# A four-part hybrid layer on one core: row variances of the feed-forward outputs on GpSimd, and every feed-forward sum begun in PSUM by VectorE

## The chip, the core and the metric

The kernel runs on one core of a Trainium2 chip. The metric is device time in microseconds (us) of one launch, the median of three runs. Everything is float32. The engines are TensorE (PE in the profile), VectorE (DVE), ScalarE (ACT), GpSimd (POOL) and SyncE (SP).

## The reference, cut to what matters

```python
def _layernorm(x, eps=1e-5):  m, v = mean(x), var(x); return (x - m) / sqrt(v + eps)
def attn(h):                  q = h @ Wq.T; return (q @ h.T) @ h            # no softmax
def ffn(t):                   x = t + relu(t @ w1[0] + b1[0]) @ w2[0] + b2[0]
                              return (x - mean(x)) * rsqrt(var(x) + 1e-5) * gamma + beta
def mix(x):                   ...   # RWKV time mixing (a scan over tokens), then channel mixing
x = hidden                                    # 8 batches of 512 rows x 128 columns
x = x + attn(_layernorm(x))
x = x + ffn(_layernorm(x))                    # called f1 in the kernel
x = x + mix(_layernorm(x))                    # called tmix and cmix in the kernel
x = x + ffn(_layernorm(x))                    # f2, with the same weights as f1
```

The feed-forward part keeps expert 0 alone, since the reference sets its weight to one. Its input t is a normed row, and its own result is normed again after t, the product and b2 are added up.

## The kernel before, in words

A tile is one of the eight batches: 512 rows, laid as 4 blocks (j) of 128 rows with 128 columns each. All eight tiles of x stay in SBUF (R0 to R7). Each tile goes through five parts: attention, f1, tmix, cmix, f2. Nothing is scheduled by a compiler: each engine has a list of calls written out by hand, in which parts of different tiles are interleaved, and each call waits on counting semaphores for what it needs. The lists end the functions of each engine. An engine takes its list strictly in order.

One feed-forward tile runs so. `normed` (ScalarE, L828) writes the normed rows `y`; `ffn_transpose` (TensorE, L1114) turns them, ScalarE copies them to `yT` (L881, L884); `hidden_up` (L1155) multiplies by W1 into four banks of PSUM, `relu` (L895) moves these to `h`. Then z = y + h @ W2 + b2 is summed up in one PSUM bank: the bank is begun with y and `ffn_down` (L1164) adds 16 products to it. There are two ways to begin it.

- Tiles in `STARTED` (f1: 0 to 3, f2: 4 to 7): VectorE's `ffn_start` (L700; for the last tile `last_start`, L707, in two halves) writes y + B2R into the bank; B2R is b2 less its mean, in every row.
- The other eight tiles: TensorE's `ffn_start` (L1275) transposes yT back into the bank, in four steps, where yT holds y + B2C since ScalarE adds the column B2C as it copies (L884). Their hidden layer takes the bias B1C = B1 - W1.T B2C instead of B1; `bias_part` (L1267) and `up_bias` (L733) make B1C once.

W2 is centred at the start (`centre_down_weights`), y is centred, and so is b2 in either form: every row of z has mean zero. The norm of z thus needs the variance alone. `z_stats` (VectorE, L440) takes `bn_stats` of the four blocks, `mean_var` (VectorE, L523) aggregates these, `z_log` (L1012) and `z_root` (L1017) on ScalarE make rs = (var + eps) ** -0.5, and `ffn_scaled` (VectorE, L560) writes zg = z * rs * gamma, which frees the bank. GpSimd adds zg to R by a DMA that accumulates (`ffn_sum`, L382), after it has added beta in the same way (`ffn_residual`, L374). Tile 0 of f1 is added by VectorE (`ffn_gain` L538, `ffn_out` L546), the last of f2 in two halves by `last_stats` to `last_out`.

The other names that the prediction uses: `gated` (VectorE, L650) is the last step of a tile's time mixing before its output product `product_o` (TensorE, L1213); `tmix_out` (L658) adds this product; `cmix_out` (L691) ends tile 7's channel mixing on VectorE. `bias_diagonal` (L717), `bias_rows` (L1258, L1259) and `bias_rows_centred` (L722 to L727) make B2R and B2C at the start. `shift`, `power` and `bias` are the three GpSimd steps of the other norms (L293, L294, L346, L350), with small 128x4 operands.

## Time and profile before

| | us |
|---|---|
| median of 3 runs | 259.32 (259.31 to 259.61) |
| the profiled execution's own time | 259.21 |
| its span, from first to last instruction | 257.4 |

| engine | busy us | share | instructions |
|---|---|---|---|
| TensorE, matmuls | 249.5 | 97% | 1504 |
| VectorE | 231.2 | 90% | 757 |
| ScalarE | 231.9 | 90% | 477 |
| GpSimd | 133.2 | 52% | 258 |

The profile comes from one execution. 1.8 us of its time lie outside the span. A matmul of float32 appears as two instructions, a transpose as one. Instructions overlap on one engine: the next starts before the one before it has ended. So what an instruction costs an engine without idle time is the distance from its start to the next start, which is shorter than its duration. DMA issues on GpSimd (L374, L382, L390, L397) take its time as well.

### The profile page before, as it was taken

To read this page: it belongs to the slowest core of one execution; us is meant where nothing else is said; L and a number is where in the kernel's file an instruction comes from. 1 tells how busy PE (TensorE), PEld (TensorE's weight loads), DVE (VectorE), ACT (ScalarE), POOL (GpSimd) and SP (SyncE) were. 2 spreads that over 40 slices of the span, in tenths; PEclk is the share of its full clock that TensorE was granted. 3 is DMA by queue.
4 is the path that set the end of the run, shared out by engine and by line. 5 is a ranking of instruction groups with operands and counts; after the bars stand their busy time and mean duration, and the time that the engine had idled before them with its cause. 6 is when DMAs were issued, how large, how long until landed. Compare 5 with 4: busy or idle time off the path is not lost.

```text
span 257.4 us, 5284 instructions
## 1 busy us (share of the span) xinstructions
PE 249.5 (97%) x1504; PEld 187.8 (73%) x1504; DVE 231.2 (90%) x757; ACT 231.9 (90%) x477; POOL 133.2 (52%) x258
## 2 busy tenths in 40 slices
PE   7899999999999999999999999999999999999991
PEld 7687778768767777668759767757848849778771
DVE  5897999999999999999999999999999995955454
ACT  3789789999999999999999999999999999895741
POOL 1656585944961974044596646636604525340640
PEclk9999999999999999999999999999999999999998
DMA  7932224013022240020763422205204424374297
GB/s 196 308 99 45 42 42 84 0 28 56 3 40 43 41 84 1 0 45 0 134 105 52 74 48 45 42 0 98 67 0 85 81 56 70 55 144 87 45 187 179
DMA packets 17772, 18.10 MB, mean 70 GB/s; under 512 B 1488, under 2 KB 11600, under 8 KB 17744
## 3 DMA queue, kind: packets, MB, share of 16 engines
q0 software_dynamic: 6480, 11.80, 27.0%
q1 hardware_dynamic: 10848, 5.84, 8.1%
q8 instruction: 12, 0.20, 0.3%
q10 hardware_dynamic: 416, 0.14, 0.2%
q14 instruction: 16, 0.13, 0.2%
HBM read 3.87 MB, written 2.10 MB: 23 GB/s over the span
## 4 chain that ended last, share of the span: by engine, by line
PE 94%; DVE 2%; DMA 1%; ACT 1%; POOL 1%; issue 0%; DVEq 0%; POOLq 0%; ACTq 0%
PE bank L1155 21%; PE bank L1164 21%; PE bank L1232 11%; PE bank L1226 11%; PE bank L1114 7%; PE bank L1213 3%; PE bank L1243 3%; PE bank L1197 3%; PE bank L1207 3%; PE bank L1202 3%; PE bank L1142 3%; PE bank L1127 2%; PE bank L1275 1%; DMA R<-in_hidden 1%; PE bank L1175 1%; PE bank L1135 1%
## 5 line engine op out<-in xcount | busy, mean ns | idle before, releaser
L1164 PEld LDWEIGHTS bank<-W,f_h 128*128 128x128 f32 x480 | 58.2, 192 | 8.7 <-issue 8.6
L1155 PE MATMUL bank<-f_yT,W 128*128 128x512 f32 x128 | 61.2, 593 | 0.0
L1164 PE MATMUL bank<-W,f_h 128*128 128x128 f32 x480 | 60.2, 275 | 0.0
L1155 PEld LDWEIGHTS bank<-f_yT,W 128*128 128x128 f32 x128 | 21.9, 190 | 16.3 <-issue 11.3
L1232 PEld LDWEIGHTS bank<-FWv,KK 128*128 128x128 f32 x256 | 30.6, 192 | 3.4 <-issue 2.3
L1226 PE MATMUL bank<-XK,FWk 128*128 128x512 f32 x64 | 32.0, 597 | 0.0
L1232 PE MATMUL bank<-FWv,KK 128*128 128x128 f32 x256 | 31.8, 275 | 0.0
L828 ACT ACTIVATE f_y<-R,f_yn_nb,f_yn_rs 128x128 f32<-128x128 f32 x64 | 26.3, 490 | 0.9 <-POOL f_yn_nb L350 0.9
L895 ACT ACTIVATE f_h<-bank,B 128x512 f32<-128x512 f32 x32 | 21.2, 681 | 5.5 <-PE bank L1155 4.2
L390 POOL DMA_DIRECT2D R<-G x7 | 6.3, 897 | 36.4 <-DVE G L686 36.4
L895 ACT ACTIVATE f_h<-bank,B1C 128x512 f32<-128x512 f32 x32 | 21.4, 682 | 0.1
L293 POOL TENSOR_TENSOR f_yn_ve<-f_yn_mv,K_EPS 128x4 f32<-128x4 f32 x16 | 7.9, 493 | 25.6 <-DVE f_yn_mv L523 25.5
L382 POOL DMA_DIRECT2D R<-f_zg x14 | 14.1, 1006 | 13.4 <-DVE f_zg L560 11.2
L956 ACT ACTIVATE KK<-KK 128x512 f32<-128x512 f32 x32 | 19.8, 637 | 0.0
L952 ACT ACTIVATE KK<-bank 128x512 f32<-128x512 f32 x32 | 18.8, 599 | 0.8 <-PE bank L1226 0.7
L346 POOL TENSOR_TENSOR f_yn_rs<-f_yn_ve,K_RSQRT 128x4 f32<-128x4 f32 x16 | 19.3, 1206 | 0.0
L560 DVE SCALAR_TENSOR_TENSOR f_zg<-bank,f_zn_rs,GAMMA 128x128 f32<-128x128 f32 x56 | 15.6, 338 | 3.2 <-issue 2.2
L374 POOL DMA_DIRECT2D R<-BETA x16 | 15.7, 1037 | 4.6 <-ACT f_y L828 4.0
L1226 PEld LDWEIGHTS bank<-XK,FWk 128*128 128x128 f32 x64 | 10.7, 190 | 8.2 <-issue 4.4
L440 DVE BATCH_NORM_STATS2 f_zn_stats<-bank 128x6 f32<-128x128 f32 x60 | 13.1, 279 | 1.7 <-PE bank L1164 1.7
L440 DVE BATCH_NORM_STATS2 f_yn_stats<-R 128x6 f32<-128x128 f32 x64 | 13.7, 275 | 0.1
L828 ACT ACTIVATE N<-R,tmix_nb,tmix_rs 128x128 f32<-128x128 f32 x32 | 13.2, 489 | 0.4 <-POOL tmix_nb L350 0.4
(159 smaller groups left out, 620.3 us busy)
## 6 DMA issues: line engine op xcount, KB each, us to landing
R<-BETA POOLq DMA_DIRECT2D x16, 256.0 KB, 3.6
R<-f_zg POOLq DMA_DIRECT2D x14, 256.0 KB, 4.0
R<-N POOLq DMA_DIRECT2D x8, 256.0 KB, 3.4
R<-in_hidden SPq DMA_DIRECT2D x7, 256.0 KB, 5.0
R<-G POOLq DMA_DIRECT2D x7, 256.0 KB, 3.4
out_x<-R SPq DMA_DIRECT2D x7, 256.0 KB, 2.3
W<-in_w SPq DMA_DIRECT2D x2, 256.0 KB, 4.5
BETA<-in_beta SPq DMA_DIRECT2D x1, 256.0 KB, 4.6
```

Source lines behind the costliest of these rows:

```text
L346: pool.tensor_tensor(n.rs[b % 2][:], n.ve[b % 2][:], K_RSQRT[:], ALU.pow).then_inc(n.scale.sem(b), 1)
L374: pool.dma_start(R[b][:], BETA[:], accum_op=ALU.add).then_inc(*f.xb.step(b))
L440: last = v.bn_stats(n.stats[b % 2][:, j, :], src[:, j, :])
L828: done = a.activation(dst[:, j, :], src[:, j, :], ACT.Identity, scale=n.rs[b % 2][:, j:j + 1], bias=n.nb[b % 2][:, j:j + 1])
L895: a.activation(at(f.h, b)[:, n, :], banks[bank][:], ACT.Relu, bias=bias[:, n:n + 1]).then_inc(f.h_ready[n], 1)
L952: a.activation(at(KK, b)[:, n, :], banks[bank][:], ACT.Relu).then_inc(square[n].sem(b), 1)
L956: a.activation(at(KK, b)[:, n, :], at(KK, b)[:, n, :], ACT.Square).then_inc(square[n].sem(b), 1)
L1114: last = t_.matmul(banks[bank][:, j * P:(j + 1) * P], src[:, j, :], IDENT[:], start=(j == 0), stop=(j == J - 1), is_transpose=True, skip_g ...
L1155: t_.matmul(banks[bank][:], W1[:, n * P:(n + 1) * P], at(f.yT, b)[:], start=True, stop=True).then_inc(f.h_psum[n], 1)
L1164: last = t_.matmul(banks[bank][:, j * C:(j + 1) * C], at(f.h, b)[:, n, j * P:(j + 1) * P], W2[:, n, :], start=False, stop=(n == H - 1), sk ...
L1226: t_.matmul(banks[bank][:], FWk[:, n * P:(n + 1) * P], at(XK2, b)[:], start=True, stop=True).then_inc(kk_psum[n], 1)
L1232: last = t_.matmul(banks[bank][:, j * C:(j + 1) * C], at(KK, b)[:, n, j * P:(j + 1) * P], FWv[:, n, :], start=(n == 0 and j == 0), stop=(n ...
```

## The change

Four edits, and new orders of the calls on all five engines.

1. `STARTED` now names all sixteen tiles. VectorE's `ffn_start` runs for f1 4 to 7 and f2 0 to 3 too; TensorE's `ffn_start`, `bias_part` and VectorE's `up_bias` are called no more.
2. `mean_var` is no longer called for the z of 15 tiles (all but the last one's halves). GpSimd's new `z_spread` takes the sums of squares out of the `bn_stats` results instead: a group of 128 columns gives two means (even and odd columns) and two sums of squares about them. Since the whole row's mean is zero, 128 times the variance is the sum of the latter two less 128 times the product of the two means. These are four 128x4 instructions.
3. `z_log` waits for `z_spread` and scales by 1/128 as it takes the logarithm.
4. `bias_diagonal` and `bias_rows` stand ahead of tile 0's attention, and tile 0's `attn_gram` ahead of its transpose.

```diff
-STARTED = {"f1": (0, 1, 2, 3), "f2": (4, 5, 6, 7)}
+STARTED = {"f1": tuple(range(BATCHES)), "f2": tuple(range(BATCHES))}
...
+            def z_spread(b, n):
+
+                pool.wait_ge(n.stats_done, b + 1)
+                if b >= 2:
+                    pool.wait_ge(*n.scale.done(b - 2, "ve"))
+                st = n.stats[b % 2]
+                pool.tensor_tensor(n.pair[b % 2][:], st[:, :, 1], st[:, :, 4], ALU.mult).then_inc(n.scale.sem(b), 1)
+                pool.tensor_tensor(n.sum[b % 2][:], st[:, :, 2], st[:, :, 5], ALU.add)
+                pool.wait_ge(*n.scale.done(b, "pair"))
+                pool.tensor_tensor(n.pair[b % 2][:], n.pair[b % 2][:], K_C[:], ALU.mult).then_inc(n.scale.sem(b), 1)
+                pool.wait_ge(*n.scale.done(b, "scaled"))
+                pool.tensor_tensor(n.spread[b % 2][:], n.sum[b % 2][:], n.pair[b % 2][:], ALU.subtract).then_inc(n.scale.sem(b), 1)
...
             def row_stats(b, n, src):
                 if b >= 2:
-                    dve.wait_ge(n.mv_ready, b - 1)
+                    if n in (f1.znorm, f2.znorm):
+                        dve.wait_ge(*n.scale.done(b - 2, "spread"))
+                    else:
+                        dve.wait_ge(n.mv_ready, b - 1)
...
             def z_log(b, f):
                 n = f.znorm
-                act.wait_ge(const_ready, 8)
-                act.wait_ge(n.mv_ready, b + 1)
+                act.wait_ge(const_ready, 9)
+                act.wait_ge(*n.scale.done(b, "spread"))
...
+                a.activation(n.ve[b % 2][:], n.spread[b % 2][:], ACT.Ln, bias=K_EPS[:, 0:1], scale=1.0 / C).then_inc(n.scale.sem(b), 1)
...
-            warm_up(0, 10)
...
-            ffn_down(0, f1, 0, 3); ffn_down(0, f1, 1, 3); ffn_down(0, f1, 2, 3); ffn_down(0, f1, 3, 3)
...
+            bias_rows(); attn_gram(0, 0); attn_transpose(0, 1); attn_proj(0, 0); attn_apply(0, 0)
```

Where the orders differ is seen in three places. Line numbers of after are those of the changed file.

VectorE from the first `bn_stats` of an f1 sum (tile 0, f1_zn_stats0) on; before:

```order
L440 BN_STATS f1_zn_stats0<-bank3 128x6 x4
L523 BN_AGGR f1_zn_mv0<-f1_zn_stats0 128x2 x4
L538 TENSOR_TENSOR f1_zg0<-bank3,GAMMA 128x512
L546 SCALAR_TENSOR_TENSOR R0<-f1_zg0,f1_zn_rs0,R0 128x128 x4
L440 BN_STATS tmix_stats0<-R0 128x6 x4
L523 BN_AGGR tmix_mv0<-tmix_stats0 128x2 x4
L529 TENSOR_TENSOR R3<-bank2,R3 128x512
L756 TENSOR_SCALAR WROW<-WROW,WDEC 128x512
L440 BN_STATS f1_yn_stats1<-R3 128x6 x4
L440 BN_STATS attn_stats1<-R7 128x6 x4
```

and after, from the two rows ahead of it:

```order
L464 BN_STATS attn_stats1<-R7 128x6 x4
L729 TENSOR_TENSOR bank4<-f1_y1,B2R 128x512
L464 BN_STATS f1_zn_stats0<-bank2 128x6 x4
L567 TENSOR_TENSOR f1_zg0<-bank2,GAMMA 128x512
L575 SCALAR_TENSOR_TENSOR R0<-f1_zg0,f1_zn_rs0,R0 128x128 x4
L464 BN_STATS tmix_stats0<-R0 128x6 x4
L547 BN_AGGR tmix_mv0<-tmix_stats0 128x2 x4
L729 TENSOR_TENSOR bank7<-f1_y2,B2R 128x512
L558 TENSOR_TENSOR R3<-bank2,R3 128x512
L464 BN_STATS f1_yn_stats1<-R3 128x6 x4
```

The aggregation of z is gone, and tile 7's attention statistics have moved ahead of z's.

VectorE at the end of tile 7's time mixing (`gated` is the row G<-EA,G); before:

```order
L631 TENSOR_TENSOR AB<-AB,EB 128x2x512
L636 TENSOR_TENSOR EA<-AB,EA 128x1024
L642 SCALAR_TENSOR_TENSOR G<-G,EA 128x512
L681 SCALAR_TENSOR_TENSOR G2<-bank5,G2 128x512
L646 SCALAR_TENSOR_TENSOR G<-bank4,G 128x512
L686 TENSOR_TENSOR G2<-bank0,G2 128x512
L650 TENSOR_TENSOR G<-EA,G 128x512
L677 SCALAR_TENSOR_TENSOR DC<-DC,VEC,XC 128x512
L700 TENSOR_TENSOR bank2<-f2_y1,B2R 128x512
L523 BN_AGGR f2_zn_mv0<-f2_zn_stats0 128x2 x4
L658 SCALAR_TENSOR_TENSOR N1<-N1,tmix_back1,bank6 128x128 x4
```

and after:

```order
L660 TENSOR_TENSOR AB<-AB,EB 128x2x512
L695 TENSOR_TENSOR DC<-XC 128x512
L665 TENSOR_TENSOR EA<-AB,EA 128x1024
L702 SCALAR_TENSOR_TENSOR XK2<-DC,VEC,XC 128x512
L671 SCALAR_TENSOR_TENSOR G<-G,EA 128x512
L710 SCALAR_TENSOR_TENSOR G2<-bank3,G2 128x512
L675 SCALAR_TENSOR_TENSOR G<-bank5,G 128x512
L715 TENSOR_TENSOR G2<-bank2,G2 128x512
L679 TENSOR_TENSOR G<-EA,G 128x512
L706 SCALAR_TENSOR_TENSOR DC<-DC,VEC,XC 128x512
L729 TENSOR_TENSOR bank3<-f2_y1,B2R 128x512
L687 SCALAR_TENSOR_TENSOR N1<-N1,tmix_back1,bank4 128x128 x4
```

Two steps of channel mixing now stand between instructions that need each other's result; the `ffn_start` behind `gated` was there before.

TensorE about tile 7's `product_o` (the row with Wo); before:

```order
L1226 MATMUL bank6<-XK2,FWk 128x512
L1226 MATMUL bank5<-XK2,FWk 128x512
L1155 MATMUL bank4<-f2_yT0,W1 128x512
L1155 MATMUL bank0<-f2_yT0,W1 128x512
L1213 MATMUL bank6<-Wo,G 128x128 x4
L1155 MATMUL bank7<-f2_yT0,W1 128x512
L1243 MATMUL bank0<-FWr,DC 128x128 x4
```

and after:

```order
L1257 MATMUL bank1<-XK2,FWk 128x512
L1257 MATMUL bank3<-XK2,FWk 128x512
L1257 MATMUL bank5<-XK2,FWk 128x512
L1257 MATMUL bank2<-XK2,FWk 128x512
L1244 MATMUL bank4<-Wo,G 128x128 x4
L1186 MATMUL bank1<-f2_yT0,W1 128x512
L1195 MATMUL bank3<-W2,f2_h 128x128 x4
L1274 MATMUL bank4<-FWr,DC 128x128 x4
```

The same products stand ahead of it and behind it as before, in another order.

## Rows read from the trace of the kernel before

**Rows 1.** The page: busy us of each engine, and the chain that ended last.
```profile
PE 249.5 (97%) x1504; PEld 187.8 (73%) x1504; DVE 231.2 (90%) x757; ACT 231.9 (90%) x477; POOL 133.2 (52%) x258
PE 94%; DVE 2%; DMA 1%; ACT 1%; POOL 1%; issue 0%; DVEq 0%; POOLq 0%; ACTq 0%
```
**Rows 2.** Windows: stretch, its us, busy us and instructions of PE, PEld, DVE, ACT, POOL; clock.
```profile
0.00:26.00 26.00, 23.38 (x151) 20.25 (x152) 19.53 (x108) 18.86 (x48) 13.18 (x48) 1.00 0.60 160
26.00:210.50 184.50, 184.47 (x1086) 134.86 (x1085) 183.21 (x530) 180.07 (x358) 102.50 (x183) 1.00 0.27 48
211.50:257.40 45.90, 40.67 (x267) 32.26 (x265) 27.45 (x120) 31.96 (x70) 16.55 (x28) 0.98 0.57 110
```
**Rows 3.** VectorE in order of time, 204 to 213 us: start, duration, instruction.
```profile
204.99 1.22 DVE L631 TENSOR_TENSOR AB<-AB,EB 128x1024 f32<-128x1024 f32 x1
206.25 1.23 DVE L636 TENSOR_TENSOR EA<-AB,EA 128x1024 f32<-128x1024 f32 x1
...
210.28 0.69 DVE L650 TENSOR_TENSOR G<-EA,G 128x512 f32<-128x512 f32 x1
210.89 0.74 DVE L677 SCALAR_TENSOR_TENSOR DC<-DC,VEC,XC 128x512 f32<-128x512 f32 x1
211.56 0.69 DVE L700 TENSOR_TENSOR bank<-f_y,B2R 128x512 f32<-128x512 f32 x1
212.16 0.37 DVE L523 BATCH_NORM_AGGREGATE f_zn_mv<-f_zn_stats 128x2 f32<-128x6 f32 x4
```
**Rows 4.** TensorE in order of time, 204 to 213 us.
```profile
204.77 0.60 PE L1114 MATMUL bank<-IDENT,f_y 128*128 128x128 f32 x4
205.21 1.91 PE L1226 MATMUL bank<-XK,FWk 128*128 128x512 f32 x4
...
211.54 1.05 PE L1213 MATMUL bank<-Wo,G 128*128 128x128 f32 x8
```
**Rows 5.** TensorE in order of time, 13 to 48 us.
```profile
13.79 0.39 PE L1258 MATMUL bank<-DIAG,MEAN 128*128 128x128 f32 x2
...
14.15 1.14 PE L1142 MATMUL bank<-PROJ,XNT 128*128 128x128 f32 x8
...
21.58 0.60 PE L1114 MATMUL bank<-IDENT,f_y 128*128 128x128 f32 x4
22.06 3.81 PE L1164 MATMUL bank<-W,f_h 128*128 128x128 f32 x32
...
46.31 0.95 PE L1267 MATMUL bank<-B2C,W 128*128 128x1 f32 x8
47.12 1.10 PE L1207 MATMUL bank<-DX,Wr 128*128 128x512 f32 x2
```
**Rows 6.** VectorE in order of time, 25 to 38 us.
```profile
25.91 0.89 DVE L440 BATCH_NORM_STATS2 f_zn_stats<-bank 128x6 f32<-128x128 f32 x4 [1.67 <-PE bank L1164]
26.83 0.38 DVE L523 BATCH_NORM_AGGREGATE f_zn_mv<-f_zn_stats 128x2 f32<-128x6 f32 x4
27.13 0.66 DVE L538 TENSOR_TENSOR f_zg<-bank,GAMMA 128x512 f32<-128x512 f32 x1
27.88 1.14 DVE L546 SCALAR_TENSOR_TENSOR R<-f_zg,f_zn_rs,R 128x128 f32<-128x128 f32 x4
...
35.47 0.66 DVE L567 TENSOR_TENSOR DX<-XA 128x512 f32<-128x512 f32 x1
36.17 0.75 DVE L573 SCALAR_TENSOR_TENSOR XK<-DX,VEC,XA 128x512 f32<-128x512 f32 x1
36.84 1.12 DVE L560 SCALAR_TENSOR_TENSOR f_zg<-bank,f_zn_rs,GAMMA 128x128 f32<-128x128 f32 x4
```
**Rows 7.** GpSimd in order of time, 30 to 36 us.
```profile
30.41 0.20 POOL L328 TENSOR_TENSOR tmix_tmp<-tmix_mv,K_EPS 128x4 f32<-128x4 f32 x1 [2.67 <-DVE tmix_mv L523]
30.57 0.20 POOL L329 TENSOR_TENSOR tmix_nm<-tmix_mv,K_NEG 128x4 f32<-128x4 f32 x1
...
32.66 0.89 POOL L374 DMA_DIRECT2D R<-BETA  x1
...
34.34 1.05 POOL L293 TENSOR_TENSOR f_yn_ve<-f_yn_mv,K_EPS 128x4 f32<-128x4 f32 x1
```
**Rows 8.** ScalarE in order of time, 27 us.
```profile
27.31 0.30 ACT L1012 ACTIVATE f_zn_ve<-f_zn_mv,K_EPS 128x4 f32<-128x4 f32 x1 [1.52 <-DVE f_zn_mv L523]
27.64 0.20 ACT L1017 ACTIVATE f_zn_rs<-f_zn_ve 128x4 f32<-128x4 f32 x1
```
**Rows 9.** Line L650, all eight: duration ns min/median/max.
```profile
L650 DVE TENSOR_TENSOR G<-EA,G x8: 658/663/693, 56.9 to 210.3; 128x512 f32<-128x512 f32 x8
```

More of the change, by code:

```diff
@@ L139, in __init__ @@
                 self.rs = copies(n + "_rs", [P, J], 2)
+                if "spread" in steps:
+                    self.pair, self.sum, self.spread = (copies(n + "_" + m, [P, J], 2) for m in ("pair", "sum", "spread"))
                 self.stats_done = sem(n + "_stats_done")
@@ new lines, in _ @@
+            mean_var(1, f2.norm); with_current(4); tmix_change(5); mean_var(6, nt); gate_sum(4); cmix_change(3)
+            mix_k(5); z_stats(7, f1, 2); cmix_k(3); gate_log(4, 5); running_max(5, 7); cgate_log(2, 1); gated(4)
+            ffn_start(1, f2, 1, cgate.done(2, "rl")); differences(5, 7); mix_v(5); cmix_gated(2, 0); mix_r(5)
+            tmix_out(4, 5); z_stats(0, f2, 3); cmix_stats(4); cmix_r(3); mean_var(4, ncm); ffn_stats(2, f2)
+            new_values(5, 4); ffn_scaled(7, f1, 2); tmix_change(6); denominator_sum(5); mean_var(2, f2.norm)
@@ new lines, in _ @@
+            first_values(5, 4); numerator_sum(5); mix_k(6); weighted(5); with_current(5); cmix_change(4); gate_sum(5)
+            cmix_k(4); mix_v(6); tmix_stats(7); gate_log(5, 7); cgate_log(3, 2); mean_var(7, nt); gated(5)
+            running_max(6, 7); cmix_gated(3, 5); differences(6, 7); tmix_out(5, 6)
+            ffn_start(2, f2, 0, square[1].done(4, "relu")); cmix_stats(5); ffn_scaled(0, f2, 3); mean_var(5, ncm)
+            ffn_stats(3, f2); mix_r(6); cmix_r(4); new_values(6, 7); mean_var(3, f2.norm); first_values(6, 7)
@@ new lines, in _ @@
+            denominator_sum(7); numerator_sum(7); weighted(7); cmix_change(6); with_current(7); cmix_k(6); gate_sum(7)
+            cgate_log(5, 3); gate_log(7, 5); cmix_gated(5, 2); gated(7); cmix_r(6)
+            ffn_start(4, f2, 3, square[0].done(6, "relu")); tmix_out(7, 4); cmix_stats(7); mean_var(7, ncm)
+            ffn_stats(5, f2); z_stats(3, f2, 7); mean_var(5, f2.norm); cmix_change(7); cmix_k(7); cgate_log(6, 4)
+            z_stats(4, f2, 3); cmix_r(7); ffn_scaled(2, f2, 0); cmix_gated(6, 6)
@@ L819, in _ @@
+            last_scaled(1, 7); last_out(0); last_out(1)
         @block.scalar
@@ L1097, in _ @@
+            relu(7, f2, 3, 6); relu(7, f2, 0, 2); z_log(6, f2); z_root(6, f2.znorm); relu(7, f2, 1, 5)
+            relu(7, f2, 2, 6); last_log(0); last_root(0); last_log(1); last_root(1)
         @block.tensor
```

524 lines of the change are left out of this document (249 added, 275 removed).

## The prediction, made before the changed kernel ran

> **What bounds the kernel now.** I read the page's busy times and chain first [rows 1]. They seem to say it all: TensorE is busy for 249.5 of 257.4 us and holds 94% of the chain that ended last. But the chain only says that TensorE never had to wait at the end of a step; two other engines are at 90%. So I read windows next [rows 2]. From 26 to 210.5 us TensorE is busy for 184.47 of 184.50 us, and VectorE for 183.21, ScalarE for 180.07. Three engines are full there, and the kernel before is a balance of three. After 211.5 us VectorE has 27.5 us of work in 45.9, ScalarE 32.0, TensorE 40.7: there TensorE alone is full.
>
> Third, I looked in order of time for the place where one kind of bound hands over to the other. VectorE's `gated` of tile 7 starts at 210.28 and the instruction behind it at 210.89; it ends at 210.97 [rows 3]. TensorE starts `product_o` of tile 7, which needs it, at 211.54 [rows 4]. The slack between them is 0.57 us, all that TensorE's queue is behind VectorE at this point. From there to the end it takes 257.4 - 211.54 = 45.9 us, of which 40.7 are TensorE's own work without a gap.
>
> So the end is: the start of `product_o` of tile 7, plus 45.9 us, if what TensorE has behind it stays the same. And its start is the later of two: TensorE's own work ahead, and VectorE's work up to `gated` (with ScalarE's, whose full stretch is as long).
>
> **The change part by part: TensorE.** It loses 8 times four transposes back. Four transposes take 205.21 - 204.77 = 0.44 us from start to start [rows 4], so 8 x 0.44 = 3.5. It loses `bias_part`, 47.12 - 46.31 = 0.8 us [rows 5]. Together 4.3 us, and all of it ahead of `product_o` of tile 7. Behind that call the new order has the same calls in both kernels: gate 7 and gate 6, the downs of f2 4, all of f2 5 to 7 and of cmix 7, the last hidden piece of f2 4. Taken alone this would let `product_o` start at 207.2.
>
> **VectorE, up to `gated` of tile 7.** I counted the calls ahead of it in both orders. Added: 8 `ffn_start`. One costs 212.16 - 211.56 = 0.60 us from start to start [rows 3], so +4.8. Removed: `mean_var` of ten z, f1 0 to 7 and f2 0 and 1 (the other five stand behind `gated`, where VectorE has time to spare), and `up_bias`, one 128x4 instruction of some 0.05. A `mean_var` costs 27.13 - 26.83 = 0.30, so ten are -3.0. All else ahead of `gated` is the same. The sum is +1.75 us: on the engine that is full from 26 to 211 us the change is a loss, since it takes out fewer short instructions there than it puts in long ones.
>
> The new order gives some of it back. Where an instruction needs the result of the one just ahead of it, it starts after that one's end: L636 starts at 206.25, 0.04 after 204.99 + 1.22. Where it doesn't, it starts before the end: L700 at 211.56, 0.07 before 210.89 + 0.74 [rows 3]. Such a pair costs 0.11 to 0.12 us. From `ffn_out` of tile 0 to `gated` of tile 7 I count 16 such pairs before and 8 after (in the second piece of the orders DC and XK2 have been put between three of them). That is 8 x 0.12 = -1.0.
>
> The start of this stretch, in three steps. (a) The bias products (14.15 - 13.79 = 0.36 us [rows 5]) move to where TensorE still waits for tile 0, and two of the four downs of f1 0 no longer wait for a relu behind the transposes of tile 1. Before, the ups end just ahead of the transposes that start at 21.58, the downs run from 22.06 and z_stats begins at 25.91 [rows 5, 6]. After, with 3.6 us of downs and 0.44 of transposes from 21.6 on, it begins at 25.6: -0.3. (b) From z_stats to `ffn_out` it was 27.88 - 25.91 = 1.97 us [rows 6]. Now GpSimd stands between. Its independent instructions start 0.15 us apart and end 0.20 after their start [rows 7], so `z_spread` of four, with two waits on itself of about 0.1, takes 0.8 us. From the start of z_log to that of `ffn_out` it was 27.88 - 27.31 = 0.57 [rows 6, 8]. With two handovers of 0.1: 25.6 + 0.9 + 0.1 + 0.8 + 0.1 + 0.6 = 28.1, so `ffn_out` starts 0.2 later than before, and VectorE idles 0.9 us ahead of it. (c) Behind `ffn_out` stand +4.8 for 8 starts, -2.7 for nine `mean_var`, -0.05, -0.8 for tile 7's attention statistics, which have moved ahead of z_stats into idle time (first piece of the orders), and +0.3 for tile 6's aggregation, which has moved behind it. That makes +1.55, and +0.55 with the pairs.
>
> `gated` of tile 7 then starts at 210.28 + 0.2 + 0.55 = 211.0 and ends at 211.7. `product_o` starts as soon as the signal is there, at 211.8, for TensorE has been waiting: 211.8 - 211.54 = +0.3. The 4.3 us taken from TensorE turn into idle time ahead of that. The end: 259.21 + 0.3 = 259.5 for an execution like the profiled one, which lies 0.1 below the median of 259.32. Against the median I forecast 259.6, and all times below are against it.
>
> **ScalarE** has the same instructions; one more relu and two fewer of cmix stand ahead of its last step for tile 7's gate. I cost it at nothing. Its cover is VectorE's own length, and if VectorE were faster, ScalarE with 180 of 184.5 us would be next.
>
> **GpSimd** gets 15 x 4 instructions. At 0.2 us each they are 12 us, 133 to 145 of 257, on an engine with gaps. The work hides, the latency need not: z_log on ScalarE and behind it `ffn_scaled` on VectorE, each with a full queue behind it, now wait for it. The shortest cover is f1 tile 1, where between z_stats and `ffn_scaled` stand the decay row, tmix_change and mix_k, some 0.5 + 0.7 + 0.67 = 1.9 us (the latter two from 35.47 to 36.84 [rows 6]), against the chain of 1.8. All others have 4 us or more. But GpSimd is not even: behind a DMA issue the same 128x4 addition took 1.05 instead of 0.20 us [rows 7]. Bounds for this wait, summed over 14 tiles: 0 if every cover holds, 14 x 0.85 = 12 us if each z_spread met such a delay without cover. I take 0 on top of tile 0's, since the covers of 4 us are above 1.8 + 2 x 0.85.
>
> VectorE's eight new starts read two tiles of SBUF. L650 does the same, and its eight took 658 to 693 ns while GpSimd was busy for 55% of the stretch [rows 2, 9]: nobody holds VectorE up. The Trainium skill (SBUF — State Buffer, "Who interferes with whom") says that a VectorE instruction with two SBUF inputs and a GpSimd instruction that reads SBUF share a read port, and whichever comes second is blocked until the first is done. By that rule each new GpSimd instruction could hold a VectorE instruction for up to its own 0.2 us; with some 40 of them ahead of `gated` and about half of VectorE's time in such instructions that would be an estimated 4 us, and 263.6 in all. The spread of 35 ns in rows 9 speaks against it for VectorE; the long GpSimd rows would be the other side of it.
>
> **The rivals.**
> A. Faster, by VectorE. Its stretch has more waste to give than my 8 pairs: it is 184.4 us from z_stats to `gated`, of which by my count 16 pairs x 0.12 and six waits of about 0.18 for other engines were waste, 3 us. With TensorE early, results lie ready and these waits (1.1 us) go too, and if tile 0's wait of 0.9 is shorter than I think, another 0.5. `gated` 1.6 earlier than forecast: 258.0. With the rest of the 3 us gone as well (2.0 behind the 1.0 that I count, and 0.3 of pairs at the start) 257.3.
> B. Faster, by TensorE: it was the bound after all, and the whole 4.3 us come out: 255.0. For it speaks the chain's 94%. Against it speaks that VectorE has no gap to shrink.
> C. Slower, by the new wait: `z_spread` comes late, because GpSimd stands in its order at a DMA issue or at a wait for someone else, and VectorE and ScalarE, both full, stand still behind `ffn_scaled` and `z_log`. It decides from the second such stall on: each costs its full length, 0.5 to 1 us. With three of 0.8: 262.0. For it: 15 new chains through an engine in strict order, whose instructions vary by a factor of five. Against: 39 norms went the same way before.
> D. Slower, by the clock. TensorE now idles 4 to 5 us ahead of 211.8. In the last stretch, where it stops some 5 us before the end, the granted clock was 0.98 on average [rows 2], so it fell from 2.4 towards 1.2 GHz there. If the idle time came in one piece, 4 us of products at half speed cost 4 us: 263.6. The Trainium skill (TensorE: Matmul & The Clock Gate, "What's actually happening") has the same: the clock is given by activity and taken back when idle. Spread over many waits, as up to 26 us where it stayed at 1.00 with 2.6 us of idle time, it costs nothing.
>
> **How the numbers follow.** Forecast (259.6, own range 258.8 to 260.4): 0.45. A 0.24, B 0.04, C 0.23, D 0.04. Differences below 0.2%, 0.5 us, can't be told from none here. The middle of the forecast's range lies within 258.8 to 259.8: I give 0.30 to same, 0.11 to slower and 0.04 to faster of its 0.45. A goes to faster but for 0.05, B to faster, C and D to slower: faster 0.27, same 0.35, slower 0.38. The range for 8 in 10 goes from 257.4 (within A; beyond it 0.08) to 262.0 (C as priced; beyond it 0.09).
>
> **What would show it.** Right: TensorE has some 4 us of waits between 26 and 212 us, most ended by VectorE; VectorE is busy without a gap over it; L679 starts at about 211.0 and L1244 at 211.8; from there to the end 45.9. Step (b) is right if VectorE idles 0.9 us ahead of L575. C would show as idle time of VectorE ahead of L589, ended by f_zn_rs, and of ScalarE ahead of f_zn_ve, ended by POOL. B would be right if VectorE had gaps and L679 started near 207. The forecast is wrong if the stretch behind `product_o` is not the same 45.9, for then the hand-over lies elsewhere.

## The result: 262.1 us, slower by 2.7, and the profile after

| | before | after |
|---|---|---|
| median, us | 259.31 | 262.06 (261.91 to 263.21, four runs) |
| profiled execution, its span | 259.21, 257.4 | 262.12, 260.3 |
| VectorE starts `ffn_out` of tile 0 | 27.88 | 27.93 |
| VectorE starts `gated` of tile 7 | 210.28 | 213.26 |
| TensorE starts `product_o` of tile 7 | 211.54 | 214.51 |
| from there to the end of the span | 45.9 | 45.8 |

The ratio is 1.0108, with an interval of 1.0089 to 1.0126: slower, and just outside the range that I gave.

The page of after, busy us and the chain that ended last. Before, TensorE held 94% of the chain [rows 1].

```profile
PE 249.0 (96%) x1464; PEld 182.6 (70%) x1464; DVE 230.5 (89%) x704; ACT 232.1 (89%) x477; POOL 152.3 (59%) x319
PE 55%; DVE 16%; ACT 12%; issue 8%; POOL 6%; DMA 1%; DVEq 0%; ACTq 0%; POOLq 0%
```

The chain now passes from engine to engine. Windows of after, with the columns of [rows 2] (behind the clock stand the DMA engines' share and GB/s):

```profile
26.00:211.50 185.50, 181.84 (x1041) 129.08 (x1039) 182.02 (x493) 178.62 (x355) 115.55 (x219) 1.00 0.26 48
211.50:260.30 48.80, 43.71 (x274) 33.54 (x272) 28.30 (x104) 34.82 (x76) 22.19 (x49) 0.97 0.51 103
```

The clock is 1.00 up to 211.5 us. In this stretch TensorE now idles 3.7 us, VectorE 3.5 and ScalarE 6.9, where it was 0.0, 1.3 and 4.4 [rows 2]. VectorE at the start of its full stretch, after (before: [rows 6]):

```profile
25.52 0.89 DVE L464 BATCH_NORM_STATS2 f_zn_stats<-bank 128x6 f32<-128x128 f32 x4 [1.79 <-PE bank L1195]
...
27.93 1.14 DVE L575 SCALAR_TENSOR_TENSOR R<-f_zg,f_zn_rs,R 128x128 f32<-128x128 f32 x4 [0.93 <-ACT f_zn_rs L1048]
...
34.14 0.89 DVE L464 BATCH_NORM_STATS2 f_zn_stats<-bank 128x6 f32<-128x128 f32 x4 [0.86 <-PE bank L1195]
...
35.73 0.69 DVE L596 TENSOR_TENSOR DX<-XA 128x512 f32<-128x512 f32 x1 [0.31 <-ACT XA L927]
```

The first two rows are steps (a) and (b) of the prediction, and they came as forecast: they start at 25.52 and 27.93 us, where I had said 25.6 and 28.1, and the wait is 0.93 us, where I had said 0.9. The other two waits are new. And VectorE and TensorE at the hand-over, after (before: [rows 3, 4]):

```profile
213.26 0.69 DVE L679 TENSOR_TENSOR G<-EA,G 128x512 f32<-128x512 f32 x1
```
```profile
210.95 3.72 PE L1257 MATMUL bank<-XK,FWk 128*128 128x512 f32 x8
214.51 1.05 PE L1244 MATMUL bank<-Wo,G 128*128 128x128 f32 x8
```

`product_o` starts 1.25 us after `gated`, by the same distance as before (1.26), and right behind TensorE's other work. So TensorE had not run ahead at all, though 4.3 us of work were taken from it.

**How TensorE's lost time is read.** The page hardly shows it: 40 instructions went, and its busy time fell by 0.5 us, since the modelled ends of matmuls cover short waits. The starts show it. In a stretch without waits a 128x512 matmul starts 0.43 us after the one before, a 128x128 one 0.11. Here is one of the two largest gaps of after (the other, at 121.6 us, is as long):

```profile
97.20 1.16 PE L1263 MATMUL bank<-FWv,KK 128*128 128x128 f32 x8
99.07 1.10 PE L1228 MATMUL bank<-XK,Wk 128*128 128x512 f32 x2 [0.71 <-DVE XK L602]
```

Eight starts at 0.11 end at 98.1; the product starts at 99.07, so nearly 1 us is lost where the row says 0.71. Summed over all starts from 26 to 212 us, TensorE lost 1.3 us before and 9.1 us after. That is 7.8 more against 4.3 of work saved: +3.5, of which `product_o` of tile 7 shows 3.0 (in the two orders TensorE also stands at different calls at 26 us). The same sum on VectorE, over distances that exceed the usual one of the same instruction by more than 0.2 us, is 0.2 us in one place before and 3.3 in six places after. Its small gaps of 0.05 to 0.2 us, among them the dependent pairs of the prediction, fell from about 3 us to about half of that. These sums are mine, from the starts in the traces; I call them lost time below.

### The profile page after: what moved, and what is told of

Same layout as the page of the kernel before. It is cut to its first block, busy times and chain, and to the rows that moved or that the text cites. A ratio compares the mean times of both kernels' runs of the same rounds, so it can differ in the third digit from the quotient of the medians.

```text
span 260.3 us, 5233 instructions
## 1 busy us (share of the span) xinstructions
PE 249.0 (96%) x1464; PEld 182.6 (70%) x1464; DVE 230.5 (89%) x704; ACT 232.1 (89%) x477; POOL 152.3 (59%) x319
## 3 DMA queue, kind: packets, MB, share of 16 engines
q0 software_dynamic: 6480, 11.80, 25.6%
## 4 chain that ended last, share of the span: by engine, by line
PE 55%; DVE 16%; ACT 12%; issue 8%; POOL 6%; DMA 1%; DVEq 0%; ACTq 0%; POOLq 0%
PE bank L1186 13%; PE bank L1195 13%; PE bank L1263 8%; PE bank L1257 6%; PE bank L1145 4%; PE bank L1228 2%; DVE f_zg L589 2%; PE bank L1274 2%; ACT EA L944 2%; PE bank L1173 1%; PE bank L1158 1%; DVE AB L655 1%; PE bank L1244 1%; ACT EA L952 1%; ACT EB L939 1%
## 5 line engine op out<-in xcount | busy, mean ns | idle before, releaser
L1195 PE MATMUL bank<-W,f_h 128*128 128x128 f32 x480 | 61.2, 276 | 0.1
L919 ACT ACTIVATE f_h<-bank,B 128x512 f32<-128x512 f32 x64 | 42.5, 681 | 7.1 <-PE bank L1186 6.1
L1257 PE MATMUL bank<-XK,FWk 128*128 128x512 f32 x64 | 31.1, 597 | 0.0
L399 POOL DMA_DIRECT2D R<-f_zg x14 | 13.2, 942 | 12.7 <-DVE f_zg L589 11.5
L297 POOL TENSOR_TENSOR f_yn_ve<-f_yn_mv,K_EPS 128x4 f32<-128x4 f32 x16 | 9.5, 592 | 18.9 <-DVE f_yn_mv L547 18.9
L589 DVE SCALAR_TENSOR_TENSOR f_zg<-bank,f_zn_rs,GAMMA 128x128 f32<-128x128 f32 x56 | 15.5, 338 | 5.4 <-issue 5.4
L391 POOL DMA_DIRECT2D R<-BETA x16 | 17.6, 1097 | 4.3 <-ACT f_y L852 3.7
L976 ACT ACTIVATE KK<-bank 128x512 f32<-128x512 f32 x32 | 18.0, 596 | 0.3 <-PE bank L1257 0.3
L363 POOL TENSOR_TENSOR f_yn_rs<-f_yn_ve,K_RSQRT 128x4 f32<-128x4 f32 x16 | 18.0, 1127 | 0.0
L332 POOL TENSOR_TENSOR tmix_tmp<-tmix_mv,K_EPS 128x4 f32<-128x4 f32 x8 | 2.3, 290 | 23.6 <-DVE tmix_mv L547 23.6
L852 ACT ACTIVATE NC<-N,cmix_nb,cmix_rs 128x128 f32<-128x128 f32 x32 | 13.2, 485 | 0.7 <-POOL cmix_nb L367 0.6
```

The costliest lines, as they stand in the source:

```text
L363: pool.tensor_tensor(n.rs[b % 2][:], n.ve[b % 2][:], K_RSQRT[:], ALU.pow).then_inc(n.scale.sem(b), 1)
L391: pool.dma_start(R[b][:], BETA[:], accum_op=ALU.add).then_inc(*f.xb.step(b))
L589: last = v.scalar_tensor_tensor(zg[:, j, :], z[:, j, :], f.znorm.rs[b % 2][:, j:j + 1], GAMMA[:], ALU.mult, ALU.mult)
L852: done = a.activation(dst[:, j, :], src[:, j, :], ACT.Identity, scale=n.rs[b % 2][:, j:j + 1], bias=n.nb[b % 2][:, j:j + 1])
L919: a.activation(at(f.h, b)[:, n, :], banks[bank][:], ACT.Relu, bias=bias[:, n:n + 1]).then_inc(f.h_ready[n], 1)
L976: a.activation(at(KK, b)[:, n, :], banks[bank][:], ACT.Relu).then_inc(square[n].sem(b), 1)
```

## The experiments

All were timed beside the kernel before, in five groups (its median was 259.25 to 259.52 in them). A difference between two runs of different groups can be off by up to 0.3 us for that reason alone; the ratios are each taken within a group. Lists of calls in the cuts below are wrapped anew, so that both sides show the same calls. "Old" and "new orders" are the call lists of the kernel before and of the changed one. "Lost" is TensorE's from 26 to 212 us; `gated` is tile 7's start.

| run | orders | sums begun by | z variance | us | ratio to before | `gated` | lost |
|---|---|---|---|---|---|---|---|
| before | old | both | VectorE | 259.3 | 1 | 210.3 | 1.3 |
| after | new | VectorE | GpSimd | 262.1 | 1.0108 | 213.3 | 9.1 |
| e1 | new | VectorE | VectorE | 263.4 | 1.0147 (1.0128 to 1.0166) | 214.2 | 9.7 |
| e2 | new | VectorE | left out | 261.1 | 1.0061 (1.0045 to 1.0077) | 211.9 | 7.6 |
| e3 | new | both | GpSimd | 262.0 | 1.0097 (1.0081 to 1.0113) | 213.7 | 5.0 |
| e4 | new | both | VectorE | 262.5 | 1.0123 (1.0105 to 1.0141) | 213.8 | 5.0 |
| e5 | old | VectorE | GpSimd | 266.5 | 1.0276 (1.0260 to 1.0292) | 217.1 | 12.5 |
| e6 | old | both | GpSimd | 262.1 | 1.0104 (1.0088 to 1.0121) | 212.2 | 3.8 |
| e7 | old | VectorE | VectorE | 265.4 | 1.0229 (1.0212 to 1.0247) | 215.5 | 10.8 |
| e8 | old | both | left out | 258.6 | 0.9973 (0.9962 to 0.9984) | 210.1 | 0.7 |
| e9 | old | transposes left out | VectorE | 259.2 | 0.9997 (0.9983 to 1.0010) | 210.0 | 4.8 |
| e10 | old | transposes left out | left out | 258.2 | 0.9966 (0.9950 to 0.9981) | 209.1 | 4.0 |
| e11 | new | transposes left out | VectorE | 261.9 | 1.0100 (1.0083 to 1.0117) | 213.2 | 7.5 |
| e12 | old | both | GpSimd for 6 tiles | 258.0 | 0.9948 (0.9930 to 0.9966) | 209.4 | 0.8 |
| e13 | new | both | left out | 261.8 | 1.0090 (1.0072 to 1.0107) | 212.9 | 4.3 |
| e14 | old | both | GpSimd for 2 tiles | 260.6 | 1.0042 (1.0027 to 1.0057) | 212.3 | 3.5 |
| e15 | new | VectorE | GpSimd for 12 tiles | 261.1 | 1.0055 (1.0042 to 1.0069) | 213.2 | 8.6 |
| e16 | new, one place put back | both | VectorE | 263.9 | 1.0176 (1.0160 to 1.0191) | 214.9 | 6.3 |
| e17 | the same | VectorE | GpSimd for 12 tiles | 264.7 | 1.0199 (1.0181 to 1.0216) | 217.3 | 12.1 |

**Undoing the parts in the new orders: e1 to e4.** e1 puts `mean_var` back behind each `z_stats` and drops `z_spread`:

```diff
-                act.wait_ge(*n.scale.done(b, "spread"))
+                act.wait_ge(n.mv_ready, b + 1)
...
-            z_stats(1, f1, 4); decay_along_tokens(); tmix_change(0); mix_k(0)
+            z_stats(1, f1, 4); decay_along_tokens(); mean_var(1, f1.znorm); tmix_change(0); mix_k(0)
```

> The changed kernel with part 2 undone: mean_var of all fifteen z is back on VectorE, right behind z_stats (one call later where that is possible), z_log reads it again, GpSimd has no z_spread. Orders otherwise those of the changed kernel. The changed kernel takes 262.1. V (VectorE's length sets the time): ten aggregations of 0.30 come back ahead of gated of tile 7, so 264 to 265. G (the new steps on GpSimd hold the other norms and z up, and these waits are the loss): VectorE's waits of 1.9 us go and pay for most of the 3.0, ScalarE's waits for POOL go too: 261 to 262.5. O (the new orders are the loss, TensorE and VectorE wait for each other by turns): about 262 to 263, with the waits of TensorE unchanged.

e2 leaves the variance out:

```diff
-                a.activation(n.ve[b % 2][:], n.spread[b % 2][:], ACT.Ln, bias=K_EPS[:, 0:1], scale=1.0 / C).then_inc(n.scale.sem(b), 1)
+                a.activation(n.ve[b % 2][:], n.stats[b % 2][:, :, 2], ACT.Ln, bias=K_EPS[:, 0:1], scale=2.0 / C).then_inc(n.scale.sem(b), 1)
```

> The changed kernel, orders and all, with the variance of fifteen z left out on every engine: z_log reads one of the bn_stats results (twice the squares of the even columns) as soon as z_stats is done. Left out: the combination of the two halves, so the output's scale is slightly another. V: nothing was taken off VectorE, so 261.5 to 262.1 (tile 0's wait of 0.9 for the handover shortens by about 0.6). G: all waits that come from GpSimd's longer queue go, 259 to 260, and the waits of ScalarE for tmix_nb, f_yn_nb at 32.7, 80.6, 148.8 are gone. O: as V.

e3 puts TensorE's `ffn_start` back, just ahead of the first down of each of the eight tiles, with `bias_part` and `up_bias`:

```diff
-STARTED = {"f1": tuple(range(BATCHES)), "f2": tuple(range(BATCHES))}
+STARTED = {"f1": (0, 1, 2, 3), "f2": (4, 5, 6, 7)}
...
-            product_r(2, 3); ffn_down(5, f1, 0, 2)
+            product_r(2, 3); ffn_start(5, f1, 2, (f1.h_ready[3], 5)); ffn_down(5, f1, 0, 2)
```

> The changed kernel with part 1 undone: eight sums are begun by TensorE's four transposes again, just ahead of their first down product; bias_part and up_bias are back; z_spread stays on GpSimd, orders otherwise those of the changed kernel. V: VectorE loses eight starts of 0.60 and gains 0.05: gated of tile 7 some 4.7 us earlier, but TensorE, which gets 4.3 us more, takes over: 258.5 to 260.5. T (TensorE is as much the bound in the changed kernel as before): its 4.3 us come on top, 265 to 266. O: 262 or more.

e4 does what e1 and e3 do:

> Both parts undone, only the new orders are left: the same instructions as the kernel before, in the orders of the changed kernel. If the orders cost nothing: 259.3. O (the new orders are the loss): 262 or more, slower by 1% than the kernel before. V and G: 259 to 260.

e1 and e2 lie in none of the ranges that I gave for them; e3 and e4 are as theory O has it, e3 at its very edge. e4 is the run that decides. It has exactly the instructions of the kernel before on every engine, and the new orders (with the bank numbers that belong to them) alone take 262.5: 3.1 us more than before, where the whole change cost 2.7. The two parts together give 0.4 us back in them, which is within the intervals. Part 2 is worth 1.3 there (e1 to after) where VectorE's length says 3.0, and part 1 costs nothing beside `z_spread` (e3 to after) and 0.9 without it (e4 to e1), where VectorE's length says 4.75. e2 says that the steps on GpSimd cost 1.0 us more than no variance at all; that is G, and about a third of what it was to explain. e4 is one way of putting the old parts into the new lists, so it prices these orders with this placement. Windows over the middle, before, e4 and after, in this order, columns as in [rows 2]:

```profile
26.00:212.00 186.00, 185.97 (x1093) 135.70 (x1092) 184.71 (x532) 181.57 (x361) 104.00 (x184) 1.00 0.27 48
```
```profile
26.00:212.00 186.00, 183.93 (x1081) 133.71 (x1080) 181.63 (x531) 179.50 (x356) 97.73 (x179) 1.00 0.27 48
```
```profile
26.00:212.00 186.00, 182.34 (x1042) 129.25 (x1041) 182.42 (x494) 179.12 (x356) 115.55 (x219) 1.00 0.26 48
```

In e4 VectorE is idle 4.4 us (before: 1.3), TensorE 2.1 (before: 0), ScalarE 6.5 (before: 4.4). No engine has become the bound; each waits for the others by turns. By stretches, before:

```profile
26.00:40.00 14.00, 14.00 (x81) 10.15 (x80) 13.48 (x57) 11.64 (x29) 9.92 (x21) 1.00 0.25 42
80.00:125.00 45.00, 45.00 (x271) 33.39 (x271) 45.00 (x127) 44.78 (x88) 21.44 (x40) 1.00 0.18 30
```

and e4:

```profile
26.00:40.00 14.00, 14.00 (x80) 9.66 (x79) 12.45 (x56) 12.39 (x31) 6.36 (x16) 1.00 0.12 20
80.00:125.00 45.00, 43.59 (x245) 30.49 (x244) 44.70 (x133) 43.90 (x85) 21.58 (x41) 1.00 0.17 30
```

and after:

```profile
26.00:40.00 14.00, 14.00 (x79) 9.53 (x78) 11.76 (x47) 11.95 (x30) 8.47 (x24) 1.00 0.11 20
80.00:125.00 45.00, 42.89 (x240) 30.12 (x240) 45.00 (x124) 43.73 (x85) 25.14 (x49) 1.00 0.16 29
155.00:214.00 59.00, 58.98 (x329) 41.31 (x328) 58.01 (x144) 58.38 (x112) 28.52 (x55) 1.00 0.30 57
```

First TensorE is full and VectorE is idle (1.5 us of 14 in e4; in after 2.2, of which 0.9 are step (b)'s wait for ScalarE). From 80 to 125 it is the other way, and from 155 on TensorE is full again. The first large wait of VectorE in e4 is the one that after has at 34.14:

```profile
32.92 0.35 DVE L524 BATCH_NORM_AGGREGATE attn_mv<-attn_stats 128x2 f32<-128x6 f32 x4
34.44 0.69 DVE L441 BATCH_NORM_STATS2 f_zn_stats<-bank 128x6 f32<-128x128 f32 x3 [1.17 <-PE bank L1165]
```

The kernel before has no wait there. Its VectorE and TensorE, and TensorE of after:

```profile
34.27 0.88 DVE L440 BATCH_NORM_STATS2 f_zn_stats<-bank 128x6 f32<-128x128 f32 x4
```
```profile
30.26 3.74 PE L1164 MATMUL bank<-W,f_h 128*128 128x128 f32 x32
```
```profile
30.36 3.73 PE L1195 MATMUL bank<-W,f_h 128*128 128x128 f32 x32
```

The new order took work of VectorE away from ahead of this call: tile 7's statistics (0.8 us) went ahead of tile 0's z, and the decay row of the scan (L756, L780 in after) went behind the call. But the call needs TensorE's downs of f1 1, which run from 30.3 to 34.0 in both kernels. So it starts at 34.27 before and at 34.14 after: what VectorE had gained came back as a wait of 0.86 us.

**The parts in the old orders: e5 to e7.** In these, VectorE's new `ffn_start` stand in its old list where TensorE began the sum 0.8 us later, and each `z_spread` stands ahead of the first GpSimd call that started after its `z_stats`:

```diff
-            z_stats(1, f1, 0); mean_var(1, f1.znorm); tmix_change(0); mix_k(0); ffn_scaled(1, f1, 0); mix_v(0)
+            z_stats(1, f1, 0); tmix_change(0); mix_k(0); ffn_scaled(1, f1, 0); mix_v(0)
...
-            shift(3, f1.norm); power(3, f1.norm); back_scale(0); bias(3, f1.norm); ffn_sum(1, f1, f1.zg); shift(6, na)
+            shift(3, f1.norm); z_spread(1, f1.znorm); power(3, f1.norm); back_scale(0); bias(3, f1.norm); ffn_sum(1, f1, f1.zg); shift(6, na)
...
-            cmix_change(0); tmix_out(1, 6); cmix_k(0); cmix_stats(1)
+            ffn_start(6, f1, 7, (f1.yT_ready, 7)); cmix_change(0); tmix_out(1, 6); cmix_k(0); cmix_stats(1)
```

> The kernel before, in its own orders, with both parts: all sixteen sums begun by VectorE, at the places in its list where it stood 0.8 us before TensorE began them, and z_spread on GpSimd ahead of the first call that started after z_stats; mean_var of z, up_bias, bias_part and the transposes back are gone. O (the new orders are the whole loss, as the last kernel, 262.5 with the old parts, says): 258.7 to 259.4, since in the new orders the two parts gave 0.4 us. V (VectorE's length, by the terms of my sum without the gains of the new order): +1.75 on VectorE, 261. G: 260.5 or more, with ScalarE waiting for POOL.

> The kernel before, in its own orders, with part 2 alone: z_spread on GpSimd in place of mean_var of fifteen z. V: VectorE loses ten aggregations of 0.30 ahead of gated of tile 7, but TensorE's queue is only 0.57 us behind it there, so at most 0.6 to 1 off: 258.4 to 259. G: no gain or a loss, 259.4 to 260.5.

> The kernel before, in its own orders, with part 1 alone: eight more ffn_start on VectorE (+4.8 us less up_bias), TensorE 4.3 us less. V: 263 to 264, as 4.75 us come on the full VectorE with only its gaps to pay from. T (TensorE is the bound): 255 to 258. If the three engines share the bound: within 1 us of 260.5.

All three are slower than the kernel before, and slower than I expected: e6 and e7 lie above every range that I gave, and e5 lies over 5 us above V's 261, where only G's open "260.5 or more" takes it in. Part 1 alone costs 5.9 us where VectorE's sum says 4.75, so more than the sum came out, not less. Part 2 alone costs 2.7 where it should have given 0.6. Both cost 7.1, so the new orders are worth 4.4 us to a kernel with both parts and cost 3.1 us to one with neither. Orders and parts can't be priced apart and added. Each of these runs has one placement of the parts in the old lists, by the rule above; another might cost less, as e12 shows for part 2.

**How the kernel before is balanced: e8 to e10.** e8 makes e2's edit in the old orders. e9 takes away the transposes that begin eight sums:

```diff
                 pe.wait_ge(f.yT_ready, b + 1)
-                for j in range(J):
-                    t_.matmul(banks[bank][:, j * C:(j + 1) * C], at(f.yT, b)[:, j * P:(j + 1) * P], IDENT[:], start=(j == 0), stop=False,
-                              is_transpose=True, skip_group_check=True)
```

> The kernel before, in its own orders, with the variance of fifteen z left out on every engine (z_log reads one of the bn_stats results): VectorE 4.5 us less, 3.0 of them ahead of gated of tile 7, nothing new on GpSimd. V: 258.4 to 258.8, where TensorE takes over after 0.57 us. If TensorE waits for VectorE in more places than the trace shows: 257 or less. If VectorE isn't a bound at all: 259.4.

> The kernel before, in its own orders, with the four transposes that begin a sum left out for eight tiles (y + b2 is missing from these sums; the first down product begins the bank; the waits stay, and VectorE's list is as before): TensorE 3.5 us less, no other engine touched. Balance (VectorE and ScalarE are as full as TensorE, taking from one alone gives nothing beyond the hand-over): 258.8 to 259.5. T (TensorE is the bound): 256.

> The kernel before, in its own orders, with both left out: the variance of fifteen z on every engine (VectorE 4.5 us less, 3.0 ahead of gated of tile 7) and the transposes that begin eight sums (TensorE 3.5 us less). If TensorE and VectorE are the pair that sets the time: 256 to 257. If ScalarE, 180 of 184.5 us busy there, is the third: 258 to 258.6, no more than leaving out the variance alone gave (258.6).

e9 refutes rival B by itself: 3.5 us less on TensorE take 0.0 us off the time (the interval of the ratio reaches from 0.4 us less to 0.3 more). TensorE turns them into lost time (1.3 to 4.8). Its chain falls from 94% to 67% while the time stays:

```profile
PE 67%; DVE 17%; issue 7%; ACT 6%; DMA 1%; POOL 1%; DVEq 0%; ACTq 0%; POOLq 0%
```

VectorE's cut gives 0.8 in e8, about the 0.57 us of slack at the hand-over. Both cuts give 1.0 in e10, so something else holds the kernel right behind them. I had named ScalarE, 180 of 184.5 us busy, but the trace of e10 doesn't single it out: from 26 to 209 us TensorE idles 1.4 us, VectorE 2.7 and ScalarE 3.7. What limits e10 stays open.

**Are the cuts worth more in the new orders? e11 and e13.** e9's and e8's edits on e4.

> The old parts in the new orders (262.5) with the same transposes left out: TensorE 3.5 us less. A (in the new orders the bound alternates: from some 155 us to gated of tile 7 TensorE runs without a stall while VectorE waits now and then, and between 40 and 125 us TensorE stalls and VectorE is full): the transposes of f1 7 and f2 0 to 3 lie on the path, those of f1 4 to 6 don't: 1 to 2 us off, 260.5 to 261.5, where the same cut in the old orders gives nearly nothing. Balance as in the old orders: 262.0 to 262.5.

> The old parts in the new orders (262.5) with the variance of fifteen z left out on every engine: VectorE 3.0 us less ahead of gated of tile 7. The same cut in the old orders gave 0.8 us. A (in the new orders the engines wait for each other by turns, VectorE being full from 40 to 150 us while TensorE stalls): VectorE's cut comes out to a larger part, 1.5 to 2.5 us, so 260.0 to 261.0. Balance as in the old orders: 0.8 off, 261.7.

e11 gave 0.6 and e13 0.7, less than theory A asked of either. The engines wait by turns, but relieving one of them is worth as little as in the old orders. So a cut on one engine alone doesn't remove the loss of the new orders.

**Which `z_spread` costs time: e14, e12, e15.** e12 lets GpSimd take six tiles, e14 two, e15 (in the new orders) twelve:

```diff
+SPREAD = {"f1_zn": (2, 3, 4, 5, 6), "f2_zn": (1,)}
...
+            def var_ready(self, b, step=3):
+                if b in self.spreads:
+                    return self.spread_steps, 3 * self.spreads.index(b) + step
+                return self.mv_ready, len([c for c in range(b + 1) if c not in self.spreads])
...
-                act.wait_ge(n.mv_ready, b + 1)
+                act.wait_ge(*n.var_ready(b))
```

> The kernel before, in its own orders, with z_spread on GpSimd for six tiles only (f1 2 to 6 and f2 1), where the run with all fifteen showed no wait behind it; mean_var stays on VectorE for f1 0, 1, 7, f2 0 and the tail. If the 2.7 us that part 2 cost in these orders came from the few tiles at which VectorE or TensorE waited for z_spread (f1 0, f1 1, f1 7): 258.6 to 259.2, as fast as with the variance left out or a little slower. If the cost is GpSimd's load everywhere: 260 or more.

> The kernel before, in its own orders, with z_spread on GpSimd for f1 0 and f1 1 only. If these two tiles, at which nothing lies between z_stats and what waits for it, made most of the loss of 2.7 us that all fifteen gave: 260.5 to 261.7, with the waits of TensorE at 27.5 and 37.1 us that the run with all fifteen shows. If the loss is GpSimd's load over the whole program: 259.2 to 259.6.

> The changed kernel (262.1) with the variance of f1 0, f1 1 and f1 7 on VectorE again, the other twelve on GpSimd. VectorE 0.9 us more by its length; if z_spread costs most at these tiles in the new orders too, the waits that go (0.9 us ahead of ffn_out, 0.5 of ScalarE) pay for it: 261.3 to 262.1. By VectorE's length alone: 262.6 to 263.

The first two tiles alone cost 1.1 us. VectorE in e14:

```profile
28.81 1.14 DVE L572 SCALAR_TENSOR_TENSOR R<-f_zg,f_zn_rs,R 128x128 f32<-128x128 f32 x4 [1.60 <-ACT f_zn_rs L1046]
...
38.65 1.12 DVE L586 SCALAR_TENSOR_TENSOR f_zg<-bank,f_zn_rs,GAMMA 128x128 f32<-128x128 f32 x4 [0.79 <-ACT f_zn_rs L1046]
```

and GpSimd ahead of the second, in the same run:

```profile
33.77 0.89 POOL L399 DMA_DIRECT2D R<-BETA  x1
34.43 1.50 POOL L386 TENSOR_TENSOR tmix_rs<-tmix_ve,K_RSQRT 128x4 f32<-128x4 f32 x1
...
36.38 0.75 POOL L362 TENSOR_TENSOR f_zn_sum<-f_zn_stats 128x4 f32<-128x4 f32 x1
37.09 0.19 POOL L364 TENSOR_TENSOR f_zn_pair<-f_zn_pair,K_C 128x4 f32<-128x4 f32 x1
37.36 0.56 POOL L366 TENSOR_TENSOR f_zn_spread<-f_zn_sum,f_zn_pair 128x4 f32<-128x4 f32 x1
```

The statistics are there at 35.9 and the result at 37.9: 2.0 us for what I had priced at 0.8. The whole chain to `ffn_scaled` takes 2.8 us, priced at 1.8, and VectorE has work for 1.5 of them (the decay row of my 1.9 stands elsewhere in the old order) and is idle for 1.3. With these tiles on VectorE and six that have cover on GpSimd, e12 takes 258.0 us: faster than both kernels, 0.5% under the kernel before, and the gain of 1.2 us is more than I expected. How much of it the six tiles explain is less clear than the median. The profiled executions of before and e12 lie 1.7 us apart: 0.4 us are there at `ffn_out`, at 27.49 us, where e12 does nothing else than the kernel before; 0.5 us come between `ffn_out` and `gated`; and 0.8 us lie behind TensorE's last product, from whose end to that of the span it takes 4.5 us in e12 and 5.3 in before. And e8, which takes away all fifteen aggregations and gives GpSimd nothing, gained less (0.8) than e12. The page of e12:

```profile
PE 248.5 (97%) x1504; PEld 187.4 (73%) x1504; DVE 230.1 (90%) x733; ACT 231.7 (91%) x477; POOL 141.4 (55%) x283
```

e15 puts three tiles back on VectorE in the new orders: 0.9 us more work on the engine that I had called the bound, and 1.0 us less time (1.4 by the ratios of after and e15), a little below my range. Its trace doesn't show this gain in the full stretch: `product_o` of tile 7 starts at 214.44 (after: 214.51), and the profiled executions differ by 0.65 us, but only behind TensorE's last product. So the 0.9 us of work cost nothing up to there; that the move itself gave the 1.0 isn't shown.

**One wait taken away: e16, e17.** The waits for the downs of f1 1 at 34 us should shorten if TensorE does them before the transposes of f1 2, as in the old orders. With these, the gram and the transposes of tile 4's attention go ahead of the first hidden piece of f1 2, also as in the old orders:

```diff
-            hidden_up(1, f1, 3, 3, (f1.h_ready[0], 2)); ffn_transpose(2, f1, 5, (proj_ready, 4))
+            hidden_up(1, f1, 3, 3, (f1.h_ready[0], 2))
...
-            ffn_down(1, f1, 1, 4); ffn_down(1, f1, 2, 4); ffn_down(1, f1, 3, 4); tmix_transpose(0, 5)
-            hidden_up(2, f1, 0, 2, x1.ready(3)); attn_gram(4, 6); attn_transpose(4, 5, (xa_ready, 1))
+            ffn_down(1, f1, 1, 4); ffn_down(1, f1, 2, 4); ffn_down(1, f1, 3, 4); tmix_transpose(0, 3, (f1.h_ready[3], 2))
+            ffn_transpose(2, f1, 5, (proj_ready, 4)); attn_gram(4, 6); attn_transpose(4, 3, (xa_ready, 1)); hidden_up(2, f1, 0, 2, x1.ready(3))
```

> The old parts in the new orders (262.5) with one place of the order put as it was before: the transposes of f1 2 behind the downs of f1 1 and tile 0's time-mixing transposes instead of ahead of them (on TensorE; on ScalarE the copy to yT goes behind it too, three bank numbers change). If VectorE's wait for the downs of f1 1 at 33 to 34 us is carried through to gated of tile 7: 0.4 us off, 262.1. If later waits swallow it, as they do whatever is added to or taken from one engine in these orders: 262.5 within 0.2.

> The same change of one place in the kernel with both parts, new orders, and the variance of f1 0, f1 1 and f1 7 on VectorE (261.1). Carried through: 260.6 to 260.8. Swallowed: 261.1.

Both went wrong: 1.4 us slower than e4 and 3.6 slower than e15, where I had expected a gain of 0.3 to 0.5 us or none. VectorE and ScalarE in e16:

```profile
33.80 0.89 DVE L441 BATCH_NORM_STATS2 f_zn_stats<-bank 128x6 f32<-128x128 f32 x4 [0.73 <-PE bank L1165]
...
38.46 1.13 DVE L561 SCALAR_TENSOR_TENSOR f_zg<-bank,f_zn_rs,GAMMA 128x128 f32<-128x128 f32 x4 [1.53 <-ACT f_zn_rs L1018]
```
```profile
37.25 0.69 ACT L896 ACTIVATE f_h<-bank,B 128x512 f32<-128x512 f32 x1 [1.35 <-issue]
37.84 0.29 ACT L1013 ACTIVATE f_zn_ve<-f_zn_mv,K_EPS 128x4 f32<-128x4 f32 x1
```

The wait for the downs fell from 1.17 to 0.73 us as meant. But a relu of f1 2, at 35.79 in e4 and now at 37.25, since its hidden piece starts at 36.14 and not at 34.68, stands ahead of z_log of f1 1 on ScalarE, and holds VectorE for 1.53. In the kernel before z_log stands ahead of that relu: e16 put back TensorE's order at this place, and left ScalarE's order new. A loss of one engine is cured at one place and comes back larger at the next. Which places of the new orders make up the 3.1 us, taken one by one, stays open.

## Why the prediction was wrong, by its own steps

- **The hand-over and the 45.9 us behind it: right.** 45.8 in after. In all nineteen profiled executions the span ends 45.1 to 46.8 us after `product_o` of tile 7, whatever came before: 40.6 to 41.4 us up to the end of TensorE's last product, and 4.4 to 6.1 behind it. So single executions can differ by over 1 us behind the hand-over alone.
- **(a) and (b): right**, to 0.1 and 0.2 us, which is within what two executions differ by at this point.
- **(c), "+0.55 with the pairs": the step that failed.** From `ffn_out` to `gated` of tile 7 VectorE takes 185.33 us, where before it took 182.40: +2.9, forecast at +0.55. Two terms of it were wrong, with opposite signs. "The new order gives some of it back ... -1.0": e4 has the old instructions in the new orders and takes 213.83 - 27.92 = 185.91, so the orders are +3.5. The pairs did go (I count 16 before and 8 after, as forecast); what I had not looked for is what else a new order brings, waits for the other engines. The "-0.8 for tile 7's attention statistics" is the plainest case: it came back as the 0.86 us of waiting at 34.14. "+1.55" for the instructions: from e4 to after it is -0.6, since what is put in falls partly into waits and the aggregations leave. The sum of a full engine's instructions holds only as long as the engine stays nearly without waits, as in e7, where this stretch grew by 5.4 us and the sum says 4.75.
- **The 4.3 us of TensorE turn into idle time: right, and too little.** They became 7.8 us of lost time. I compared the two lists of TensorE for what stands ahead of and behind one call, and not for when each call's operands are there. That the order of three engines without slack costs nothing was an assumption without a row.
- **GpSimd, "0 on top of tile 0's": wrong, by up to 1.0 us** (after to e2; this includes what e2 saves at tile 0). This is rival C, right in kind and about a third of the loss; that the measured 262.1 lies at its 262.0 is luck. Its rows are not those that I named: VectorE doesn't wait at L589 in the full stretch. The waits sit at tile 0 and, through GpSimd's longer queue, at other norms: ScalarE waits 1.4 us for `tmix_nb`, where before it waited 0.4 (us in total, times, longest; after, 26 to 212 us):

```profile
ACT N L852 <- POOL tmix_nb L367: 1.4, 2, 0.9
```

e6 and e14 show C in the old orders, where it costs 2.7 and 1.1 us and where I had not asked. One row was read wrongly: the addition of 1.05 us in [rows 7] doesn't stand right behind the DMA issue. A power on GpSimd (L361, from 33.32 on) of 1.89 us lies between them.
- **Rivals A, B, D: wrong.** A needed VectorE's waits to go, and they grew (its 257.3 also leaves out the 0.5 us of tile 0's wait that its 258.0 counts); e9 refutes B; the granted clock was 1.00 up to 211.5 us (D).
- **That VectorE reads are held up by GpSimd** (the estimate of 263.6): not so. The eight L679 took

```profile
L679 DVE TENSOR_TENSOR G<-EA,G x8: 647/662/693, 57.2 to 213.3; 128x512 f32<-128x512 f32 x8
```

as before [rows 9], with GpSimd busy for 62% of the stretch, where before it was 56%. It is the other way round, as the next section but one shows.
